# A patch attention and two transformer layers: tile 1's projection in banks of its own, weights loaded late, and one written order for the loop's end and the feed-forward part

## What is computed

```python
xn = _layernorm(x)
x = x + _L0_attn_ref(xn, ...) + _L0_ffn_ref(xn, ...)

# _L0_attn_ref: 13 blocks of 40 tokens, each two interleaved patches of 20; 16 heads of 8
dots = einsum('brhsd,brhtd->brhst', q, k) * scale; out = softmax(dots) @ v
return scatter(out) @ Wout.T + bout

# _L0_ffn_ref, two layers (8 heads of 64, window 64, HID 341):
h = shift_token(x)                     # second half of the features is one token late
q, k, v = split(h @ wqkv)
q = l2norm(q) * qs; k = l2norm(k) * ksc; q, k = rotary_xpos(q, k)
x = x + local_attention(q, k, v) @ wo  # each window looks at itself and the one before
h = layernorm(shift_token(x)) * lg + lb
a, g = split(h @ w1 + b1)
x = x + (a * gelu(g)) @ w2 + b2
```

## Time and profile before

| | us |
|---|---|
| Time, median of 3 runs | 389.63 |
| Lowest and highest | 387.52, 389.82 |
| The profiled execution's own time | 390.88 |
| Its span | 389.1 |
| TensorE busy | 348.4 (90%) |
| ScalarE, VectorE, GpSimd busy | 291.1, 267.7, 257.9 |
| Mean granted TensorE clock | 0.98 of 2.4 GHz |

### The profile page before, as it was taken

The page is one execution under the profiler, slowest core; times in us unless marked ns, Lnnn a source line. Parts: engine busy times, 40 slices in busy tenths (PEclk is TensorE's granted clock), DMA queues, the critical chain, the costliest instruction groups (busy, mean ns, idle before and its releaser), DMA issues. The chain is left out here.

```text
span 389.1 us, 10787 instructions
## 1 busy us (share of the span) xinstructions
PE 348.4 (90%) x4007; PEld 265.4 (68%) x4007; DVE 267.7 (69%) x470; ACT 291.1 (75%) x887; POOL 257.9 (66%) x248
## 2 busy tenths in 40 slices
PE   1858779999999999988897869999999999988995
PEld 1646557888888888655454548888888888665562
DVE  4546767788878878466775676887888788365453
ACT  2556378999998999975467686899999989973620
POOL 2997479999999999720056588888998898410000
PEclk9998899999999999999999898999999999999998
DMA  6975032322322232215100122223222222200001
GB/s 192 363 153 182 3 123 56 76 56 62 72 62 49 62 77 56 49 36 182 50 0 0 28 55 47 52 63 77 55 65 62 68 58 63 60 12 7 27 27 54
DMA packets 35298, 27.63 MB, mean 71 GB/s; under 512 B 19077, under 2 KB 29231, under 8 KB 34735
## 3 DMA queue, kind: packets, MB, share of 16 engines
q1 hardware_dynamic: 34959, 26.49, 25.7%
q10 hardware_dynamic: 288, 0.46, 0.4%
HBM read 9.64 MB, written 1.05 MB: 27 GB/s over the span
## 5 line engine op out<-in xcount | busy, mean ns | idle before, releaser
L1111 ACT ACTIVATE probs<-ps,neg_max 128x128 f32<-128x128 f32 x256 | 90.0, 377 | 2.2 <-DVE neg_max L1316 1.2
L620 POOL TENSOR_TENSOR qkn<-work 128x512 f32<-128x512 f32 x64 | 80.6, 1282 | 15.4 <-DVE work L1272 5.5
L634 POOL TENSOR_TENSOR probs_n<-probs,row_inv 128x512 f32<-128x512 f32 x64 | 66.6, 1042 | 16.8 <-DVE row_inv L1321 14.6
L628 POOL TENSOR_TENSOR qkn<-qkn,rnorm 128x512 f32<-128x512 f32 x64 | 65.5, 1046 | 15.8 <-ACT rnorm L1067 15.1
L1111 ACT ACTIVATION_READ_ACCUMULATOR probs<-ps,neg_max 128x1 f32 x256 | 55.1, 215 | 0.0
L1060 ACT ACTIVATE work<-ps 128x1024 f32<-128x1024 f32 x32 | 32.8, 1026 | 22.0 <-issue 12.6
L1316 DVE TENSOR_REDUCE neg_max<-ps 128x4 f32<-128x512 f32 x64 | 41.0, 682 | 6.0 <-PE ps L834 6.0
L1262 DVE TENSOR_REDUCE ss_pair<-work 128x16 f32<-128x1024 f32 x32 | 39.0, 1220 | 8.0 <-ACT work L1060 6.1
L189 PE MATMUL ps<-wqkv_hi,h_hi 128*128 128x512 f32 x96 | 42.4, 442 | 1.6 <-ACT work L1060 1.6
L813 PE MATMUL ps<-small,qkn 128*128 128x128 f32 x256 | 37.1, 281 | 4.7 <-POOL qkn L628 4.6
L848 PE MATMUL ps<-small,probs_n 128*128 128x128 f32 x256 | 36.7, 282 | 5.1 <-POOL probs_n L634 2.8
(11 more groups left out here) (129 smaller groups left out, 758.3 us busy)
## 6 DMA issues: line engine op xcount, KB each, us to landing
v_off<-v_tok SPq DMA_DIRECT2D x64, 128.0 KB, 2.3
k_t<-k_t SPq DMA_DIRECT2D x30, 128.0 KB, 2.3
cos_w<-in_cos_t SPq DMA_DIRECT2D x2, 1024.0 KB, 8.0
sin_w<-in_sin_t SPq DMA_DIRECT2D x2, 1024.0 KB, 10.4
x_shift<-x SPq DMA_DIRECT2D x64, 32.0 KB, 1.9
x_raw<-in_x SPq DMA_DIRECT2D x4, 256.0 KB, 4.5
x<-xin SPq DMA_DIRECT2D x8, 128.0 KB, 5.5
out<-o_t SPq DMA_DIRECT2D x4, 256.0 KB, 2.3
```

The source lines that it names most:

```text
L620: pool.tensor_tensor(to, first, second[:, :, ::-1, :], ALU.add).then_inc(rot_summed, 1)
L628: pool.tensor_tensor(of, of, rnorm[:, part * HEADS:(part + 1) * HEADS].unsqueeze(2) .broadcast_to([P, HEADS, DH]), ALU.mult).then_inc(rot_ ...
L634: pool.tensor_tensor(probs_n[:, 4 * g:4 * g + 4, :], probs[:, 4 * g:4 * g + 4, :], row_inv[:, 4 * g:4 * g + 4].unsqueeze(2).broadcast_to([ ...
L1111: e = act.activation(probs[:, k, :], s_ps[g][:, cw * P:(cw + 1) * P], ACT.Exp, bias=neg_max[:, k:k + 1], accum_out=row_sum[:, k:k + 1])
```

## The change

*First part.* The loads of wo, a_wout, w2 and vectors go behind layer 1's wqkv. Patch chunk 1 is projected and taken in step 1 instead of 0; the two halves of wqkv are rounded in steps 0 and 2, the inputs in steps 2, 4, 5, 6, the masks cast in step 3 and w1 in step 7; turned inputs 2 and 3 come in steps 3 and 4. Tile 1 is projected into banks 2 and 3 directly behind tile 0; ScalarE squares both one after the other, VectorE sums both before it rotates tile 1, and project_v(0) waits for that rotation. GpSimd splits input span 0 before it scales the sine table.

*Loop's end and feed-forward part.* The tile loop ends with step 14. All that came after is written out once per engine. centered(0) stands at the end of step 13, centered(1) of step 14; the spans' norms have PSUM banks 0, 2, 0, 0. The gate and linear pairs alternate between banks 3, 4 and 6, 7. Hidden and gelu buffers take turns in q_t, k_t, v_off and probs_t. The tables are issued in step 14 of layer 0 instead of behind the loop. GpSimd no longer splits spans 2 and 3 of layer 1's input; ScalarE rounds them in quarters (64x256) and VectorE splits them, four behind the feed-forward part, four in steps 1 to 4. In layer 1's last span w2's products, the addition, turning, the last addition and the store go in two halves of 256 tokens.

SyncE:

```diff
             shift_input(0)
             shift_input(1)
+            shift_input(2)
+            shift_input(3)
+            sp.wait_ge(xn_tr, SPANS)
+            sp.dma_start(w1_raw, w1.rearrange("l p n -> p l n")).then_inc(w1_in, 16)
+            sp.wait_ge(masks_done, 1)
+            sp.dma_start(wqkv_raw[1], wqkv[1]).then_inc(wqkv_in[1], 16)
             sp.dma_start(wo_s[:], wo.rearrange("l (c p) n -> p l c n", p=P)).then_inc(w_in, 16)
...
+                    if t == TILES - 2 and layer < LAYERS - 1:
+                        sp.wait_ge(rot_done, 2 * TILES * (layer + 1))
+                        sp.dma_start(cos_w[:], cos_d).then_inc(cos_in, 16)
+                        sp.dma_start(sin_w[:], sin_d).then_inc(sin_in, 16)
```

TensorE, first part:

```diff
+        def qk_of(n):
+            return bank(2, 2) if n == 1 else bank(0, 2)
...
                     project_qk(0, 0)
+                    project_qk(0, 1)
             over_patches(pe, patch_step, in_front)
             turn_patch_out(0)
-            project_qk(0, 1)
...
                 def project_v(n):
                     after(pe, v_evac, n)
+                    if n == 0:
+                        pe.wait_ge(rot_done, 4)
```

TensorE, loop's end and feed-forward part (`gates(0, 0)` waits for all exps of the layer):

```diff
+                    if t == TILES - 3:
+                        centered(0)
+                    if t == TILES - 2:
+                        centered(1)
+                over_tiles(pe, step, TILES - 1)
...
+                scores(last, 1)
+                centered(2)
+                project_out(last - 2)
+                variance(1)
+                weigh_values(last - 1, 0)
...
+                gates(0, 0)
+                turn_probs(last, 0, True)
+                turn_probs(last, 1, True)
+                variance(2)
+                project_out(last - 1)
+                gates(0, 1)
+                weigh_values(last, 1)
+                project_out(last)
+                gates(0, 2)
+                gates(1, 0)
+                centered(3)
+                gates(1, 1)
+                variance(3)
+                feed_out(0)
+                for j in range(1, SPANS):
+                    if j > 1:
+                        gates(j, 1)
+                    gates(j, 2)
+                    if layer < LAYERS - 1 and j >= SPANS - 2:
...
+                        project_qk(layer + 1, last + 1 + j - (SPANS - 2))
+                    if j < SPANS - 1:
+                        gates(j + 1, 0)
+                    if layer == LAYERS - 1:
+                        turn_out(j - 1)
+                    if layer == LAYERS - 1 and j == SPANS - 1:
+                        feed_out_last()
+                        turn_out_last()
+                    else:
+                        feed_out(j)
```

ScalarE:

```diff
+                if t == A_STEPS:
                     act.wait_ge(w1_in, 16)
...
             norms(0)
+            norms(1)
             inverse_norms(0)
...
+                    if t == TILES - 2:
+                        square(0)
                     if there(t):
                         exps(n, 0)
                         exps(n, 1)
...
                     if layer > 0 and t == -1:
-                        round_input(layer, SPANS - 1)
+                        for q in range(4):
+                            round_quarter(3, q)
...
+                square(1)
+                exps(last, 0)
+                square(2)
+                exps(last, 1)
+                norm_rstd(1)
+                take_o(last - 1)
+                take_probs(last, 1)
+                norm_rstd(2)
                 act.preload_act_table_set("gelu_and_others")
```

VectorE, first part:

```diff
             sum_squares(0)
+            sum_squares(1)
             put_patches(0)
             rotate(1, 1, cos_w)
             rotate(1, 1, sin_w)
```

VectorE, loop and feed-forward part:

```diff
+                    if layer > 0 and 1 <= t <= 4:
+                        split_quarter(t + 3)
+                    if t == TILES - 2:
+                        normalize(0)
...
+                hidden(1, 0)
+                add_out(0)
+                hidden(1, 1)
+                normalize(SPANS - 1)
+                if layer < LAYERS - 1:
+                    scale_table(layer + 1, cos_w, 1)
+                split_normalized(SPANS - 1)
+                hidden(1, 2)
+                if layer < LAYERS - 1:
+                    scale_table(layer + 1, sin_w, 0)
+                    scale_table(layer + 1, sin_w, 1)
...
+                    add_out(3)
+                    for i in range(4):
+                        split_quarter(i)
```

GpSimd:

```diff
             split_wqkv()
+            split_first(0)
             scale_table(sin_w, sin_in)
...
-                    split_input(layer, SPANS - 2)
-                    pool.wait_ge(h_split, rounded(layer, SPANS - 2))
```

More of the change, by code:

```diff
@@ L1428, in _ @@
[L1428 to L1431 removed]
+                    else:
+                        dve.scalar_tensor_tensor(sum_t, ffn_ps, b2_out[:], of, ALU.add, ALU.add).then_inc(x2_done, 1)
+                last = TILES * (layer + 1) - 1
+                maxima(last, 0)
+                maxima(last, 1)
+                residual(last - 2, TILES - 3)
+                invert(last, 0)
+                split_normalized(0)
@@ new lines, in _ @@
+                hidden(2, 0)
+                add_out(1)
+                hidden(2, 1)
+                hidden(2, 2)
+                if layer < LAYERS - 1:
+                    rotate(last + 1, 0, cos_w)
+                    rotate(last + 1, 0, sin_w)
+                else:
+                    put_out(1)
+                hidden(3, 0)
+                add_out(2)
+                if layer < LAYERS - 1:
+                    sum_squares(last + 1)
+                hidden(3, 1)
+                hidden(3, 2)
```

465 lines of the change are left out of this document (272 added, 193 removed).

## The result

| | before | after |
|---|---|---|
| Time, median of 20 runs each (us) | 389.23 | 390.85 |
| Lowest and highest | 386.42, 391.24 | 389.57, 392.62 |
| The profiled execution's time, its span | 390.88, 389.1 | 392.04, 390.1 |
| Mean granted TensorE clock in it | 0.980 | 0.972 |

What follows compares the result with a forecast made beforehand. TensorE is 90% busy, but a ScalarE-VectorE round trip paces the tile loop and the joints hold loose time. Gains of 1.3 (start), 3.6 (loop's end to layer 1's loop) and 1.3 (end) make 389.63 - 6.2 = 383.4 us, range 378 to 388.5.

Steps and rivals of the forecast that it cites:

- the stall and its clock: Patch scores: late weight loads remove TensorE's 3.07 us "issue" gap and 1.0 us of low clock, 4.1 us gained.
- (1): Rival, first part: the stall stays or moves with the weights, costing 3.1 + 1.0, time 387.5 us; chance 0.13.
- (4): Rival: TensorE's stall multiplies as instructions queue behind tables and weights, 4.1 us each, time 395.7 us; chance 0.06.
- Walking every engine's queue forward: Patch steps: queues followed from 13.54 us with present durations; the new order starts tile 0's projection 2.0 us earlier.
- S: Start of tile 0's projection, forecast at about 33.4 us instead of 39.49.
- own banks: Tile 0's projection to first exps: project_v(0) waits for tile 1's rotation; 17.9 us plus 1.1 low clock, now 14.3.
- the loop's end: Last tiles of the loop: centered products before the scores lose 1.9 us, won back by gates at 172.4 instead of 177.39.
- I take 0.5 here: Layer 0's feed-forward part: GpSimd's input split meeting VectorE costs 0.5 us, from a range of 0 to 1.4.
- VectorE's quarters 0.36, one per tile: Layer 1's loop: four quarter splits enter VectorE's round trip, 0.36 us each, 1.4 us lost in sum.
- Rival (2): Layer 1's quarter splits each wait for a 1.3 us GpSimd instruction, 5.2 in all, time 388.6 us; chance 0.08.
- the tail: After the last product of layer 1's last span: halved additions, turns and store end 1.0 us sooner.
- Rival (3): Loop's end onward: in-order waits push the gates back, only 1.6 us gained there, time 386.7 us; chance 0.09.

Runs made afterwards that it cites:

- the first run: Kernel before with only the loads of wo, a_wout, w2 and vectors moved behind layer 1's wqkv: 386.99 us, ratio 0.9927.
- the last kernel: The placed run with span 0's cast one gelu earlier and VectorE's sine-table products one by one behind hidden(2,0) and hidden(2,1): 374.66 us, 0.9665.
- the base: Changed kernel with the first part of before (order, banks) but late weight loads, so new loop's end and feed-forward part: 384.36 us, 0.9884.
- the placed run: The base with layer 1's quarters spread over tiles 0 to 8 where engines waited, and span 0's cast two gelus later: 378.53 us, 0.9717.

## Why the prediction was wrong

*Right: the stall and its clock.* The "issue" gap of 3.07 us went with the late loads (after, and the first run) and is there in both kernels with early ones (3.07 and 2.25 us). Rivals (1) and (4) fall for the changed kernel. What the prediction didn't see is that the gap has a fixed place: in the traces that have it, it comes before the 219th of TensorE's matmuls, and a smaller one (0.40 to 0.95 us) in most traces before the 467th; in one kernel with another order of instructions one of 0.51 us stands before the 343rd. These places are 124 matmuls apart. With late loads it was gone in fourteen of sixteen traces, 0.24 us in one and 1.44 us in the last kernel, where the DMA share from 20 to 24 us was only 0.16. So moving the weights makes it rarer and shorter, but doesn't remove its cause. The fixed, even places speak for instructions that come late; that stays an inference. By the Trainium skill (Runtime: NRT & Kernel Launch, Instruction fetch mechanics), which calls such a crossing mostly hidden, the first run would have gained nothing; it gained 4.8 us at the first exps.

*Wrong: "Walking every engine's queue forward", the order worth 2.0.* This is the step that failed. S was to be 33.4 and is 37.68. The walk has the groups of patch scores at 13.5, 15.9 and 19.3; they begin at 13.59, 16.03 and 23.18, so nearly the whole error of 4.3 us lies in one step. There the first weighing doesn't start right behind its copy: it waits for chunk 1's evictions, which in the new order end 22.6 us into the span. In the traces the order costs 1.3 to 3.2 us instead of giving 2.0 (37.68 against 34.98 and 34.52, with old banks 36.40 against 35.14, which is within the unevenness of S). The times show a smaller loss in the same three pairs, 0.4, 1.7 and 0.9 us at the medians; how much of S in the trace of after is that one execution stays open. With the late loads alone S would have been 34.7. In the traces this step is 4.3 of the 7.2 us between forecast and measurement.

*Right: own banks.* S to exps was to be 19.0 and is 19.13. The loss was counted correctly and hidden in a sum that came out positive. Two small errors cancel in it: the rotation of tile 1 ended at S + 12.9 (13.3 forecast), and the low clock cost the values and turns behind it some 1.5 us (1.1 forecast; an estimate from 1.42 and 1.91 us here against 0.78 and 1.04 at full clock).

*Right: the loop's end.* 1.9 per layer forecast, 1.52 in layer 0 and 1.65 in layer 1 measured, and the gates 3.64 us behind the exps (3.5 forecast).

*Mis-sized: "I take 0.5 here", the port in the feed-forward part.* VectorE's two instructions lost 1.06 and 0.95 us beside GpSimd's 3.55, and TensorE waited 2.66 us. The part took 42.48 instead of 41.5. By the Trainium skill (SBUF — State Buffer, Who interferes with whom) the ports that the two engines share are an exclusive lock, and the second to come waits. The rows agree: the cast ended 0.29 us and the split 0.55 us after the GpSimd instruction beside which each began. The prediction counted one meeting at 0.5 us where two stood on the path.

*Mis-sized: the quarters.* "VectorE's quarters 0.36, one per tile" left out that the first four stand in front of tile 16's exps on both engines: the entry took 8.06 us, not 7.0. In the loop four quarters (0.41 us each) lengthened the distances from tile 17 to tile 21 by 1.8 us (1.4 forecast). The distance before them, 8.53 us, holds no quarter of VectorE's; there the granted clock was 0.64, and it is 1.1 longer than plain, which the prediction had at nothing. Together the five distances took 40.16 us, 2.9 over the plain 37.3, where the bubble of before had made 40.05; so the whole gain of 3.0 went. With the quarters placed in gaps, and full clock, the same five take 37.22 us. Rival (2) was right for two of the four quarters in the entry (1.0 us each), not in the loop.

*Right: the tail* (1.1 for 1.0; the last piece as a whole -3.36 for -3.2). Rival (3) was wrong: the schedule does overlap; the new end alone is worth 2.6 us at the median.

## What to carry to other kernels

In this kernel small work spread over the loop cost nothing in slots where its engine was seen to wait; at the end of a step the same eight quarters cost 0.4 to 0.6 us a tile. Before banks are split to let two projections run ahead, look at which later instruction then needs the bank, and what stands behind it in the queue. When a change has several parts, each with a gain and a loss of its own, the sum tells little: here late loads and the new end each win about 2.5 us, own banks (nearly 6 us) and the patch order give them back, and three changes of place in one kernel win 8.5 more by the ratios (0.9884 to 0.9665). And before a gain is read from a single trace, look at a second trace of the same code: what looked like 1.2 us here was the base's own unevenness.

## What the runs showed of the hardware

A stall of TensorE marked "issue", 3.07 and 2.25 us long, was gone in fourteen of sixteen traces of kernels in which loads of another engine's queue were moved some 10 us later (0.24 and 1.44 us in the other two), and always stood before the same matmul. VectorE's 128x512 cast took 1.48 instead of 0.42 us and two of its 64x256 subtractions 1.37 and 1.40 instead of 0.41 beside GpSimd's two-input instructions; in the last kernel it was GpSimd's subtraction that took 2.41 instead of 1.27 beside VectorE's table product. After TensorE had been busy for only 5.47 of 8.06 us the next 8 us had a granted clock of 0.65 (its levels are 1.2 and 2.4 GHz), while after 7.17 busy of 7.90 us it kept 1.00:

```profile
208.00:215.90 7.90, 7.17 (x62) 4.77 (x61) 5.14 (x7) 3.53 (x8) 4.54 (x4) 1.00 0.13 30
```

A wait can thus be paid in part a second time: behind the 2.09 us at 22.78 the products of L728 took 1.92 instead of 1.04 us, and behind the 2.06 us of the placed run the clock was 0.74.
